# Score-operand loads of a split-bf16 attention: 12 loads a sequence into 48 or 32 partitions in place of 16 loads into 16

## What is computed

```
xh = x.reshape(B, N, 16, 16)                      # 16 heads of 16 features
q = einsum('bnhd,hed->bnhe', xh, Wq)
attn = softmax(4 * einsum('bnhe,bmhe->bhnm', q, q))
res = einsum('bhnm,bmhe->bnhe', attn, q)
y = res.reshape(B, N, D) @ Wp.T + bp
```

## Time and profile before

| what | value |
|---|---|
| time, median of 3 runs | 1540.07 us (1535.97 to 1540.96) |
| profiled execution: own time / span | 1534.83 us / 1532.8 us |
| PE busy | 1176.3 us (77%) |
| DVE busy | 705.4 us (46%) |
| ACT busy | 574.2 us (37%) |
| POOL busy | 316.4 us (21%) |
| granted PE clock, mean | 0.889 |
| DMA, mean over the span | 66 GB/s |
| loads of `a_left` / `a_right` | 64 / 64 of 128 KB |

### The profile page before, as it was taken

One profiled execution on the slowest core, in us unless ns is written; L12 is line 12 of the kernel. 1 busy time (PEld: TensorE's weight loads), 2 busy tenths in 40 slices (PEclk: granted clock), 3 DMA queues, 4 the chain that ended last, 5 costly groups with the idle time before them and its releaser, 6 DMA issues. The chain is left out here.

```text
span 1532.8 us, 16799 instructions
## 1 busy us (share of the span) xinstructions
PE 1176.3 (77%) x4789; PEld 670.1 (44%) x4789; DVE 705.4 (46%) x1941; ACT 574.2 (37%) x925; POOL 316.4 (21%) x321
## 2 busy tenths in 40 slices
PE   2565999999999999999998383289995714527772
PEld 2432444444444444444444262156663513316552
DVE  1115555654455665445562456276662714512221
ACT  1234445555445555544452021145553100004431
POOL 6600000000000000000000102100001255536764
PEclk9777999999999999999999776679998766659997
DMA  1020001211101101120011100797620021139997
GB/s 16 7 84 0 31 8 59 72 66 38 58 24 68 45 38 58 45 92 5 34 38 38 53 1 28 139 131 105 99 37 24 35 82 44 37 111 211 224 220 133
DMA packets 59012, 101.05 MB, mean 66 GB/s; under 512 B 12202, under 2 KB 39284, under 8 KB 58706
## 3 DMA queue, kind: packets, MB, share of 16 engines
q1 hardware_dynamic: 38786, 59.81, 17.2%
q0 software_dynamic: 20176, 40.65, 10.0%
HBM read 59.40 MB, written 53.00 MB: 73 GB/s over the span
## 5 line engine op out<-in xcount | busy, mean ns | idle before, releaser
L428 PE MATMUL b_ring<-b_H,b_w 128*128 128x512 f32 x512 | 224.8, 592 | 0.0
L428 PE MATMUL b_ring<-b_X1T,b_w 128*128 128x512 f32 x512 | 223.4, 594 | 0.0
L428 PE MATMUL b_ring<-XT,b_wqkv 128*128 128x512 f32 x384 | 174.3, 598 | 7.4 <-DMA b_wqkv<-in_wqkv 7.4
L622 POOL TENSOR_TENSOR b_rstd<-b_veps,b_mhalf 128x4 f32<-128x4 f32 x32 | 32.6, 1017 | 706.5 <-DVE b_veps L69 706.5
L428 PEld LDWEIGHTS b_ring<-b_X1T,b_w 128*128 128x128 f32 x512 | 96.4, 191 | 116.2 <-issue 109.5
L428 PEld LDWEIGHTS b_ring<-b_H,b_w 128*128 128x128 f32 x512 | 96.1, 190 | 115.3 <-issue 115.3
L578 ACT ACTIVATE b_H<-b_ring,b_cur 128x512 f32<-128x512 f32 x128 | 87.9, 687 | 76.8 <-PE b_ring L428 69.7
L1401 DVE TENSOR_REDUCE a_nmax<-a_pA 128x2 f32<-128x512 f32 x128 | 84.9, 689 | 66.1 <-PE a_pA L1262 65.4
L428 PEld LDWEIGHTS b_ring<-XT,b_wqkv 128*128 128x128 f32 x384 | 71.2, 192 | 85.9 <-issue 78.1
L679 DVE RECIPROCAL b_rec<-b_den 128x1024 f32<-128x1024 f32 x16 | 104.8, 6553 | 0.6
L1631 POOL DMA_INDIRECT xe<-m_row,m_idx x84 | 83.0, 988 | 83.8 <-issue 83.8
(11 more groups left out here) (282 smaller groups left out, 1846.1 us busy)
## 6 DMA issues: line engine op xcount, KB each, us to landing
xe<-b_nil POOLq DMA_DIRECT2D x16, 1284.0 KB, 5.4
x_wt<-in_wexp SPq DMA_DIRECT2D x32, 384.0 KB
x_rows<-xe SPq DMA_DIRECT2D x32, 321.0 KB
b_w<-in_w SPq DMA_DIRECT2D x8, 1024.0 KB, 5.4
a_left<-qparts SPq DMA_DIRECT2D x64, 128.0 KB, 5.4
a_right<-qparts SPq DMA_DIRECT2D x64, 128.0 KB, 8.8
b_wqkv<-in_wqkv SPq DMA_DIRECT2D x4, 768.0 KB, 4.8
qparts<-q_part SPq DMA_DIRECT2D x24, 128.0 KB, 2.0
```

The source lines that it names most:

```text
L428: last = pe.matmul(bank[:, :], lhsT(k), rhs(k), start=(k == 0), stop=(k == n_k - 1))
```

## The change

`qparts` is now in the order sequence, half, part, row, token, so that the parts of one half lie behind each other. The pairs are put in another order: first factor 0 with second factors 0, 1, 2; then 1 with 0, 1, 2; then 2 with 0, 1. They are the same eight pairs. A group of pairs is 48, 48 or 32 partitions. For each group and half one transfer brings the second factors (parts 0 up to `count`, rows that lie behind each other in `qparts`) into `a_right`, and one brings the first factor into `a_left`, its 16 rows read `count` times through a broadcast. That is 12 transfers a sequence, eight of 192 KB and four of 128 KB, each with one run of 4096 bytes a partition. The bytes of a sequence stay 2 MB. PE waits for 12 landed transfers in place of 16. No instruction of PE, DVE, ACT or POOL is added, removed or moved.

```diff
-LEFT = (0, 0, 1, 1, 0, 2, 1, 2)
-RIGHT = (0, 1, 0, 1, 2, 0, 2, 1)
+PAIRS = ((0, 3), (1, 3), (2, 2))
...
-                        sp.dma_start(g["qparts"][c * CH // SEQ:(c + 1) * CH // SEQ, i, k, :, :].rearrange("s p t -> p s t"),
+                        sp.dma_start(g["qparts"][c * CH // SEQ:(c + 1) * CH // SEQ, k, i, :, :].rearrange("s p t -> p s t"),
...
-                for side, parts in ((left, LEFT), (right, RIGHT)):
-                    for b, part in enumerate(parts):
-                        sp.dma_start(side[b * DH:(b + 1) * DH, n % PACKS, :, :].rearrange("r (k h) t -> r k (h t)", k=KD),
-                                     g["qparts"][n, part].rearrange("k (r h) t -> r k (h t)", r=DH))\
+                for part, count in PAIRS:
+                    at = slice(part * SPLIT * DH, (part * SPLIT + count) * DH)
+                    for k in range(KD):
+                        hd = slice(k * (HEADS // KD), (k + 1) * (HEADS // KD))
+                        sp.dma_start(right[at, n % PACKS, hd, :].rearrange("r h t -> r (h t)"),
+                                     g["qparts"][n, k, 0:count].rearrange("s (r h) t -> (s r) (h t)", r=DH))\
                             .then_inc(s_pk[n % PACKS], 16)
+                        sp.dma_start(left[at, n % PACKS, hd, :].rearrange("r h t -> r (h t)"),
+                                     g["qparts"][n, k, part].rearrange("(r h) t -> r (h t)", r=DH).unsqueeze(0)
+                                     .to_broadcast([count, DH, HEADS // KD * SEQ])).then_inc(s_pk[n % PACKS], 16)
...
-                    pe.wait_ge(s_pk[slot], 16 * 16 * (l + i // PACKS + 1))
+                    pe.wait_ge(s_pk[slot], 16 * 2 * KD * len(PAIRS) * (l + i // PACKS + 1))
...
-        g["qparts"] = nc.dram_tensor("qparts", (SEQS, SPLIT, KD, P, SEQ), BF16, kind="Internal").ap()
+        g["qparts"] = nc.dram_tensor("qparts", (SEQS, KD, SPLIT, P, SEQ), BF16, kind="Internal").ap()
```

## The result

| | before | after |
|---|---|---|
| median (8 runs each, side by side) | 1538.68 us (1533.59 to 1547.32) | 1557.17 us (1553.42 to 1559.05) |
| ratio to before | | 1.0105 (95%: 1.0087 to 1.0123) |
| profiled execution: own time / span | 1534.83 / 1532.8 us | 1557.43 / 1555.4 us |
| first load of the phase to next phase's first load | 198.85 us | 216.17 us |

A forecast was written before the change was run, and what follows sets the result against it. The prediction took first-sequence loads as the bound at the start of the attention phase and PE's own work from body 1 on. Terms 7.0 + 3.5 + 2.3 + 1.0 = 13.8, say +14 us on 1540.07: 1554 us, range 1545 to 1568.

The forecast's parts named there:

- few engines, each fast: Loads of the attention phase: copies outermost confine left loads to three or two engines at 25.7 GB/s each; +14 us, chance 0.82.
- Sequence 0: Start of the attention phase: ready 24.3 us after the first load's issue in place of 17.27, +7.0 us.
- Sequence 1: Second sequence's loads: ready 18.1 us after the first sequence in place of 14.58, +3.5 us.
- The new wait after body 0: Third sequence lands 18.1 us after the second, while body 0 needs only 15.83: a new wait, +2.3 us.
- Sequence 3: Its loads land 18.1 us after the preceding sequence's, inside a body of 20.50 us: no cost.
- Sequences 4 to 7: Later bodies: loads may land past the 21.5 us free, paid at two of four; 0 to 4.8, taken as +1 us.
- PE's clock: Body 0: clock rises 2.8 us into it as before, no cost taken; staying low throughout would be +13 us less 2.3.
- Nothing else moves: End of the attention phase: the router's first load comes only as much later as the last body does; no further cost.
- both that kept all engines busy: Left loads use all engines: either faster, 1531.5 us, chance 0.08, or limited by reads at the source, 1540 us, chance 0.04.
- the first of them: Left loads on all engines at about twice today's rate: first sequence ready after 10.3 us, -8.5 us, 1531.5 us, chance 0.08.
- The slow-engine rival: Few engines carry left loads, each held up: at 8.6 GB/s sequences 53 us apart, 1816 us; half way +68; chance 0.06.
- What would show it: Expected signs: about 40 us idle before first matmuls, three waits or more; DMA share 0.2 to 0.3, 60 to 110 GB/s.

The follow-up runs named there:

- e8: The change once more on the second chip, against the kernel before: 1525.58 us in a single run, ratio 1.015, no interval.
- e1: The change with rows outermost and copies inside in the loads of both sides: 1534.03 us, ratio 0.9963 to the kernel before.
- e3: The change with its broadcast left loads kept, but right loads into 16 partitions each as before: 1588.33 us, ratio 1.0321 to the kernel before.
- e6: The change with copies outermost in only two of three groups, rows outermost in the third: 1509.94 us, ratio 1.0045 to before, second chip.
- e5: e1 with all loads of one half of the heads first and separate semaphores per half: 1494.09 us, ratio 0.9936 to before, second chip.
- e7: The change with copies outermost in only one group, rows outermost in the others: 1505.13 us, ratio 1.0005 to before, second chip.
- e2: The change with its wide right loads kept, but left loads into 16 partitions each as before: 1535.53 us, ratio 0.9985 to the kernel before.
- e4: The kernel before with each load's 16 partitions strided by 8 on both sides: 1533.52 us, ratio 0.9971 to the kernel before.

## Why the prediction was right

The forecast and its case (few engines, each fast) held. Its sum of 13.8 us is to be read against 17.3 for the phase, of which 14.8 go with the loads and 2.5 were not foreseen; both lie near the measured 16 us. By its steps:

1. *Sequence 0*: 24.3 us forecast, 23.6 measured, +6.3 for +7.0. The way there was less good. The 36 issues were to be over in 16.8 us and the crowding with them; they took 46.2. Against that, an engine made 19.5 GB/s from 988 to 996 (125 at a share of 0.40), near the 20 assumed. A disturbance taken as short was long, and the engines that carry the loss were slowed little by it (0.19 us a row in place of 0.16): that 24.3 came so near to 23.6 is in part luck.
2. *Sequence 1*: 18.1 us apart forecast, 19.6 measured, +5.0 for +3.5. This term was mis-sized: it took an undisturbed engine, while right loads were still being issued through the whole of it. Sequence 2 comes 17.86 after sequence 1, near the pace that was forecast.
3. *The new wait after body 0*: +2.3 forecast, +2.0 measured. Of it PE waits 0.79 us; the rest is step 6.
4. *Sequence 3*: nothing, and the body before 1060.91 has no wait.
5. *Sequences 4 to 7*: paid at two bodies of the four, as forecast, 1.4 us for 1. The +1 was a choice from 0 to 4.8; in e8 the same two bodies cost 2.8, and the clock 1.7 more.
6. *PE's clock*: the granted clock stayed at its lower level (0.50) for 5.2 us of body 0 in place of 2.8, so body 0's work took 17.07 us in place of 15.83. As the step says, the wait of step 3 would have been there anyway and covers it. But e1, without that wait, pays: its clock rises 5.6 us into body 0, which lasts 17.15 us. Part of what it gains in loads goes there.
7. *Nothing else moves*: wrong, by the 2.5 us of the phase's tail. The clock fell before the last projections were done: the window from 1180 holds the same 74 matmuls as one of the kernel before from 1163.3, with a clock of 0.77 against 1.00.

```profile
1163.30:1176.10 12.80, 9.10 (x74) 5.20 (x70) 2.97 (x10) 3.92 (x8) 0.00 (x0) 1.00 0.00 1
```

Of the nine kernels' profiles and that of e8, the long tail (50.9 to 51.3 us) is in the change, in e1, e3 and e8, the short one (48.4) in the others. It does not follow the idle engines: e1 keeps all busy and has it, e6 leaves many idle (share 0.52 from 978 to 992) and has the short one. What sets it stays open.

Of the rivals, both that kept all engines busy fall by the share of 0.17 to 0.40, and e1 shows that the first of them was right in kind about what all engines would give: ready after 13.0 us (10.3 forecast), -5.7 in place of -8.5. Its "twice today's rate" is what it had too high: 12.8 GB/s a busy engine, 1.5 times. The slow-engine rival falls by 25 GB/s a busy engine. What it describes, sequences further apart than a body of 20.5 us, e3 came near: 24.2 once, and every second body late.

"What would show it" held with one exception: about 40 us idle (40.9) in three waits or more (five), the later bodies near 20.5; but the share was 0.40 at first, with 125 GB/s, and 0.17 later, with 68, where 0.2 to 0.3 and 60 to 110 were given: rights filled the other engines for longer at first, and nothing filled them later. Whether the left loads landed later than the rights can't be read, as the profile gives no landing times for the loads of this kernel.

## What to carry to other kernels

Before a load is made wider, look at how its outermost step is dealt to the engines: here fewer and larger loads lose with a broadcast of three copies outermost, and win with the same copies one level in. Then read DMA share and GB/s together: a share near 1 at a low rate says that engines are held up (spread the partitions), a low share at 25 GB/s a busy engine says that too few of them work. And of these kernels e5, which asks for half of the operands first, has the shortest first wait.

## What was not expected

- SP is held when its loads are uneven: issues of 1.2 to 3.1 us from 986.93 on, also in e3, e6 and e7, but none among the first 36 of before, e1, e2, e4 and e5, which queue as many bytes on all engines. Later in the phase single issues over 1 us (up to 1.93) stand in those kernels too, and the longest is 5.61, in e3. What depth sets it wasn't tried.
- The form of a load changes its issue: 0.42 us for 16 partitions in a row, 0.59 for the same strided, 0.71 (median) for the change's left load with its copies and 0.43 for its right load, 0.59 for e1's.
- PE's clock came to its upper level at different points of the same body 0: 2.8 us into it before, 5.2 after, 5.6 in e1.
